# Second edge stage of a graph network kernel: linear maps written edge-major, values weighted on VectorE, the group's maxima transposed right behind the radial weights

## The reference, cut to what matters

```python
ms = src_s[edge_src] + dst_s[edge_dst]
mv = src_v[edge_src] + dst_v[edge_dst]
w1, w2, w3, w4, w5 = split(h @ rw3 + roff)            # radial weights of the edge
o0a, o0b = w1 * ms, w4 * einsum('eud,ed->eu', mv, Y1) / SQ3
o1a, o1b, o1c = (w2 * ms) x Y1, w3 * mv, w5 * cross(mv, Y1) / SQ2
ls, lv = eq_lin([o0a, o0b], [o1a, o1b, o1c], lin_ws, lin_bs, lin_wv)
alpha, vs, vv = ls[:, :64], ls[:, 64:], lv            # 8 heads
a = einsum('ehk,hk->eh', smooth_leaky(alpha), alpha_dot)
a = exp(a - segment_max(a, edge_dst)[edge_dst])
ns = segment_sum(vs * a, edge_dst); nv = segment_sum(vv * a, edge_dst)
```

## Time and profile before

| quantity | value |
|---|---|
| median of three runs | 9799.34 us |
| profiled execution, its own time | 9813.87 us |
| its span | 9812.0 us |
| TensorE busy over the span | 8373.1 us (85%) |
| VectorE busy | 7735.9 us (79%) |
| GpSimd busy | 7372.6 us (75%) |
| ScalarE busy | 4874.4 us (50%) |
| granted TensorE clock, mean | 0.944 |

### The profile page before, as it was taken

One profiled execution on the slowest core, in us unless ns is written; L12 is line 12 of the kernel. 1 busy time (PEld: TensorE's weight loads), 2 busy tenths in 40 slices (PEclk: granted clock), 3 DMA queues, 4 the chain that ended last, 5 costly groups with the idle time before them and its releaser, 6 DMA issues. The chain is left out here.

```text
span 9812.0 us, 193495 instructions
## 1 busy us (share of the span) xinstructions
PE 8373.1 (85%) x35878; PEld 5079.2 (52%) x35878; DVE 7735.9 (79%) x14864; ACT 4874.4 (50%) x9073; POOL 7372.6 (75%) x4571
## 2 busy tenths in 40 slices
PE   0788888888888869999985999999999999998588
PEld 0444444444444422222222777777777777777233
DVE  3177777777777768888886999999999999998465
ACT  0176666666666631121121555555555555555355
POOL 4378888888888878778774888888888888886331
PEclk9599999999999989999997999999999999999799
DMA  5578888888888877778773666666666666665222
GB/s 208 180 161 167 167 168 166 167 167 167 167 167 167 167 213 275 267 271 282 264 270 109 136 137 144 137 143 137 144 138 144 138 142 137 144 137 122 59 70 52
DMA packets 1235170, 1618.04 MB, mean 165 GB/s; under 512 B 222610, under 2 KB 1010589, under 8 KB 1178973
## 3 DMA queue, kind: packets, MB, share of 16 engines
q1 hardware_dynamic: 758950, 1273.86, 40.0%
q0 software_dynamic: 475584, 338.58, 27.1%
HBM read 1533.79 MB, written 444.07 MB: 202 GB/s over the span
## 5 line engine op out<-in xcount | busy, mean ns | idle before, releaser
L1952 POOL DMA_INDIRECT e_m<-TS,e_at x1568 | 2631.8, 1678 | 583.7 <-issue 461.4
L442 POOL DMA_INDIRECT sums<-e_total,e_place x1568 | 2506.9, 1599 | 565.9 <-DMA sums<-e_total,e_place 314.5
L579 PE MATMUL ps<-e_win,e_pick 128*128 128x448 f32 x3136 | 1325.8, 568 | 165.0 <-DVE e_u L476 97.0
L579 PEld LDWEIGHTS ps<-e_win,e_pick 128*128 128x128 f32 x3136 | 612.5, 201 | 921.6 <-issue 864.1
L2275 ACT ACTIVATE e_dT<-ps 128x512 f32<-128x512 f32 x1176 | 660.0, 596 | 495.5 <-PE ps L2149 340.1
L2275 ACT ACTIVATE e_oT<-ps 128x512 f32<-128x512 f32 x784 | 468.9, 598 | 615.1 <-PE ps L2177 373.2
L742 DVE SCALAR_TENSOR_TENSOR r_y<-ps,w_rb,r_rstd 128x512 f32<-128x512 f32 x394 | 295.6, 750 | 579.9 <-issue 533.2
L1096 POOL TENSOR_TENSOR n_zv<-n_zv,n_ast 128x1536 f32<-128x1536 f32 x200 | 703.6, 3518 | 36.6 <-DMA n_zv<-in_x_groups 22.5
L1936 POOL TENSOR_TENSOR e_val<-e_val 128x640 f32<-128x640 f32 x392 | 670.9, 1712 | 61.9 <-ACT e_val L2252 61.9
L2018 DVE TENSOR_TENSOR e_q<-e_row,dstI 128x512 f32<-128x512 int32 x392 | 704.2, 1796 | 13.3 <-PE ps L2163 13.3
L711 PE MATMUL ps<-r_sq,w_avg 128*128 128x512 f32 x788 | 458.1, 666 | 277.4 <-issue 277.4
(11 more groups left out here) (448 smaller groups left out, 19299.8 us busy)
## 6 DMA issues: line engine op xcount, KB each, us to landing
e_win<-T SPq DMA_DIRECT2D x1568, 168.0 KB
n_z<-in_x_groups SPq DMA_DIRECT2D x400, 512.0 KB
n_zv<-in_x_groups SPq DMA_DIRECT2D x800, 192.0 KB
TOT<-e_tot SPq DMA_DIRECT2D x392, 352.0 KB, 2.6
e_row<-in_src_rows SPq DMA_DIRECT2D x98, 1024.0 KB
e_local<-LR SPq DMA_DIRECT2D x196, 512.0 KB
e_row<-in_dst_rows SPq DMA_DIRECT2D x98, 1024.0 KB
e_win<-TD SPq DMA_DIRECT2D x1568, 60.0 KB
```

Of the source, the lines that this page charges most:

```text
L442: pool.indirect_dma_start(sums[c], bass.IndirectOffsetOnAxis(ap=place[:, r % 4, c:c + 1], axis=0), total[:, r % 4, c, 0:MSG0], None, compu ...
L579: pe.matmul(g[:, c, :], pick[:, p, R * c:R * c + R], win[:, s, c, :], start=True, stop=True).then_inc(spread, 1)
L1952: pool.indirect_dma_start(m_[:, r % 4, c, :], None, TS, bass.IndirectOffsetOnAxis(ap=at[:, gp, col:col + 1], axis=0), compute_op=ALU.add). ...
```

## The change

Three things change, all in `layer1_edges`.

1. The maps take the transposed products as the stationary operand and the map's weights as the moving one, tile by tile: four products of 128 columns instead of one of 512. The result is edge-major at once, in two PSUM banks of its own (4 for scalars, 5 for vectors). `turn_back`, its eight transposes and two of ScalarE's five copies are gone. The scalar map now stands between the second and the third `turn`. ScalarE takes tanh and scalar values of step i within step i.
2. `weighted` moves from GpSimd's list to the head of VectorE's step, for step i-6. VectorE's `results` are put in another order.
3. `tops_down` moves from behind the third `turn` to right behind `weights`, ahead of the first `turn`. `weigh_up` moves one step later on ScalarE, from r % 4 == 1 (between copies) to r % 4 == 2 (behind both `keep_far`).

```diff
             def _(pool):
...
-                        if not i.before(8):
-                            weighted(i, 8)
             def _(dve):
...
+                def weighted(i):
+                    j = i.r - 6
+                    slot, gp = j % STEPS, j % STEPS // 4
+                    gate(dve, k)
+                    dve.wait_ge(exped, i.uses(2, j // 4 + 1))
+                    u = val[:, gp, 4 * (slot % 4):4 * (slot % 4) + 4].rearrange("r c (h x) -> r (c h) x", x=SEG)
+                    dve.tensor_tensor(u[:, :, 1:SEG], u[:, :, 1:SEG], bc(u[:, :, 0], SEG - 1, 2), ALU.mult
+                                      ).then_inc(u_ready, 1)
...
+                        if not i.before(6):
+                            weighted(i)
                         if more:
                             sums(after)
                 def map_scalars(i):
                     gate(pe, k)
-                    pe.wait_ge(kept, i.n(5, 2))
-                    pe.matmul(ps[:, bank(i, 5), :], W["la"][:].rearrange("u a h x -> u (a h x)"), dT[:, 0, :], start=True, stop=True
-                              ).then_inc(turned, 1)
+                    pe.wait_ge(kept, i.n(3, 1))
+                    if not i.before(1):
+                        gate(pe, k)
+                        pe.wait_ge(outs, i.n(2))
+                        gate(pe, k)
+                        pe.wait_ge(silued, i.n(2, -1))
+                    for c in range(GT):
+                        last = pe.matmul(scalar_out4[:, c], dT[:, 0, R * c:R * c + R],
+                                         W["la"][:].rearrange("u a h x -> u (a h x)"), start=True, stop=True)
+                    last.then_inc(mapped, 1)
...
-                def turn_back(i, j):
...
+                        if r % 4 == 1 and not i.before(5):
+                            tops_down(i)
                         gate(pe, k)
                         pe.wait_ge(d_ready, i.n(1, 1))
                         turn(i, 0)
                         turn(i, 1)
+                        map_scalars(i)
+                        turn(i, 2)
                         if not i.before(6):
                             totals(i, 0)
-                        turn(i, 2)
-                        if r % 4 == 1 and not i.before(5):
-                            tops_down(i)
-                        map_scalars(i)
+                        map_vectors(i)
                         if not i.before(6):
                             totals(i, 1)
-                        map_vectors(i)
             def _(act):
...
                             keep_far(i.plus(3), 0, far2(i, 0))
                             keep_far(i.plus(3), 1, far2(i, 1))
-                        if not i.before(1):
-                            results(i.plus(-1))
+                        if r % 4 == 2 and not i.before(6):
+                            weigh_up(i.plus(-1))
                         keep(i, 0)
                         keep(i, 1)
+                        keep(i, 2)
+                        results(i)
                         if not i.before(6):
                             keep_totals(i, 0)
-                        keep(i, 2)
-                        keep(i, 3)
-                        if not i.before(6):
                             keep_totals(i, 1)
-                        if r % 4 == 1 and not i.before(5):
-                            weigh_up(i)
-                        keep(i, 4)
```

More of the change, by code:

```diff
@@ L1810, in bank @@
         def bank(i, j):
[L1811 removed]
+            return 2 + (5 * i.r + j) % 2
         def far2(i, half):
@@ L1928, in _ @@
             def _(pool):
-                def weighted(i, back):
-                    j = i.r - back
-                    slot, gp = j % STEPS, j % STEPS // 4
-                    gate(pool, k)
-                    pool.wait_ge(exped, i.uses(2, j // 4 + 1))
-                    u = val[:, gp, 4 * (slot % 4):4 * (slot % 4) + 4].rearrange("r c (h x) -> r (c h) x", x=SEG)
-                    pool.tensor_tensor(u[:, :, 1:SEG], u[:, :, 1:SEG], bc(u[:, :, 0], SEG - 1, 2), ALU.mult
-                                       ).then_inc(u_ready, 1)
                 def body(t):
@@ L1953, in body @@
                                 ap=at[:, gp, col:col + 1], axis=0), compute_op=ALU.add).then_inc(rows_here[r % 4], 16)
-                        if not i.before(8):
-                            weighted(i, 8)
                 passes(pool, body)
-                for r in range(8):
-                    weighted(At(PASSES, r), 8)
             @block.vector
@@ L2026, in results @@
                     dve.wait_ge(outs, i.n(2, 2))
+                    s3 = silu[:, p].rearrange("r c (h x) -> r c h x", h=HEADS)
+                    dve.scalar_tensor_tensor(out=silu[:, p], in0=silu[:, p], scalar=1.5, in1=alpha4, op0=ALU.add, op1=ALU.mult
+                                             ).then_inc(silued, 1)
+                    gate(dve, k)
+                    dve.wait_ge(mapped, i.n(2, 2))
                     for x in range(3):
@@ L2031, in results @@
                     last.then_inc(by_y, 1)
-                    s3 = silu[:, p].rearrange("r c (h x) -> r c h x", h=HEADS)
-                    dve.scalar_tensor_tensor(out=silu[:, p], in0=silu[:, p], scalar=1.5, in1=alpha4, op0=ALU.add, op1=ALU.mult
-                                             ).then_inc(silued, 1)
+                    gate(dve, k)
+                    dve.wait_ge(silued, i.n(2, 1))
+                    dve.tensor_tensor(silu[:, p], silu[:, p], bc(W["ad"][0:R, :], GT, 1), ALU.mult).then_inc(silued, 1)
                     gate(dve, k)
@@ L2109, in _ @@
                 for r in range(5):
+                    weighted(At(PASSES, r))
                     members(At(PASSES, r))
+                weighted(At(PASSES, 5))
             @block.tensor
@@ L2168, in map_scalars @@
                     gate(pe, k)
[L2169 to L2171 removed]
+                    pe.wait_ge(kept, i.n(3, 1))
[8 more added lines that the diff above has]
+                    last.then_inc(mapped, 1)
                 def map_vectors(i):
                     gate(pe, k)
[L2175 to L2183 removed]
+                    pe.wait_ge(kept, i.n(3, 3))
+                    if not i.before(1):
                         gate(pe, k)
@@ L2186, in turn_back @@
                     for c in range(GT):
-                        last = pe.transpose(out4[:, c, 128 * j:128 * j + 128], oT[:, j, R * c:R * c + R], I[:])
+                        pe.matmul(vector_out4[:, c], dT[:, 1, R * c:R * c + R], W["lb"][:].rearrange("u h x -> u (h x)"),
+                                  start=True, stop=False)
+                        last = pe.matmul(vector_out4[:, c], dT[:, 2, R * c:R * c + R],
+                                         W["lc"][:].rearrange("u h x -> u (h x)"), start=False, stop=True)
                     last.then_inc(mapped, 1)
@@ L2237, in _ @@
                 passes(pe, body)
-                for j in range(2):
-                    turn_back(At(PASSES - 1, STEPS - 1), j)
                 logits_up(At(PASSES, 0))
@@ L2325, in _ @@
                 passes(act, body)
-                results(At(PASSES - 1, STEPS - 1))
                 weigh_up(At(PASSES, 1))
```

40 lines of the change are left out of this document (12 added, 28 removed).

## The result

The changed kernel took 10093.15 us (median of four runs, 10083.39 to 10113.04), the kernel before, beside it on the same chip, 9799.04 us. The ratio is 1.0301, with a 95% interval from 1.0283 to 1.0319: 3.0% slower. The forecast had the side right (+0.3%) and the size wrong; 10093 lies above its range of 9700 to 9930.

A forecast was written before the change was run, and what follows sets the result against it. GpSimd's list was taken to bound the kernel at 37.7 us a group; after the change VectorE's 34.44 plus a 3.51 us stall made 38.0. 9813.9 + 29 - 2 = 9841 profiled, forecast 9827 us (+0.3%), range 9700 to 9930.

The forecast's parts named there:

- VectorE's own list, 34.4 us a group: VectorE's work per group of four steps, 4 x 8.13 + 1.92 us, forecast as the longest list, 3.3 less than 37.7.
- the membership back at 0.60 us a slot: `members` on VectorE, 1818 ns in the mean before, was to take 0.60 us without the weighting's reads on GpSimd.
- VectorE blocked by the DMAs (10160): Rival: `members` stays at 1.74 us beside GpSimd's indirect DMAs, 3.4 us a group more, 10160 us; chance 0.05.
- the weight loads open (10240): Rival: 18 more weight loads on TensorE add 2.0 us a step, a group of 42 us, 10240 us; chance 0.04.
- The chain from the scan to the weighting, 8.53 us: From second scan's end through TensorE and ScalarE to the exponential at VectorE: 8.53 us against 5.02 of work, 3.5 us stall.
- It is in time by 0.7 us: TensorE was to reach `tops_down` at 42.9 us, ahead of the next scan's end at 43.6.
- the round behind it: TensorE's way from one step's map to the next step's, summed from its own work to 8.52 us.
- fourth rival: TensorE comes late to the scans, by windows' DMA or slower maps: up to 1 us a group, 9925 us; chance 0.12.
- wait for the exponential: VectorE stands ahead of the weighting in a group's third step until ScalarE's exponential is done: 3.5 us a group.
- first rival: The exponential reaches VectorE within 5.02 us of the scan, group 34.4 us, 9480 us; chance of 9720 or less 0.15.
- GpSimd as the bound of the kernel before: GpSimd's list of four indirect DMAs and one weighting a step was taken as the longest, at 37.7 us a group.

The follow-up runs named there:

- e3: Changed kernel with SyncE's store of the totals one step later (step i-7 instead of i-6): 9968.60 us, ratio 1.0156 to the kernel before.
- e13: Changed kernel with both halves of the totals, and ScalarE's copy of the first, back in their places of before: 9891.01 us, ratio 1.0048.
- e6: Changed kernel with the weighting just ahead of `weigh` and the store of the totals one step later: 9688.71 us, ratio 0.9863 to the kernel before.
- e5: Kernel before with only the weighting moved from GpSimd to the head of VectorE's step, for step i-6: 9649.61 us, ratio 0.9828.
- e12: Changed kernel with weighting just ahead of `weigh`, totals' store one step later, exponential back in the group's second step: 9686.52 us, ratio 0.9872.
- e14: Changed kernel with the totals back in their places of before, weighting just ahead of `weigh`, and store one step later: 9721.73 us, ratio 0.9875.
- e9: Kernel before with only the edge-major maps and their step order; weighting on GpSimd, maxima and exponential in their old places: 10030.05 us, ratio 1.0225.
- e4: Changed kernel with the weighting back on GpSimd, for step i-8: 9943.43 us, ratio 1.0129 to the kernel before.

## Why the prediction was wrong

- **VectorE's own list, 34.4 us a group: right within 0.3.** In the window 5430 to 9100 of the changed profile VectorE was busy 3064.55 us in 357 weightings' time, 34.3 us a group. From start to start it is 40.90 - 5.68 - 0.53 = 34.7 us, the group less the waits at the weighting and the shift. The list leaves out the idle time that stands once in a turn of the loop, 70.2 / 94.5 = 0.7 us a group ahead of L1980 before and 0.4 ahead of the weighting now. The largest term in it, the membership back at 0.60 us a slot, came out (682 ns, 680 forecast). The weighting took 823 ns (810 forecast). The two rivals that hung on these, VectorE blocked by the DMAs (10160) and the weight loads open (10240), did not occur: twelve products of the vector map took from 7404.75 to 7406.09, 0.11 us each, as forecast. The rule that the prediction took from the Trainium skill (TensorE: Matmul & The Clock Gate, "The mechanism"), that a weight load overlaps running products only when the row groups differ, is not borne out by these rows; the same section also lets a load into the background weight buffer run ahead, which the prediction left out. The Trainium skill's rule on two SBUF inputs beside a GpSimd instruction that reads SBUF (SBUF — State Buffer, "Who interferes with whom") agrees with the membership's 1818 and 682 ns.
- **The chain from the scan to the weighting, 8.53 us: right where its start was.** The group at 7380 has 8.52 us, but it is one of four in 84 in which TensorE is in time. From the transpose of the maxima to the weighting are 8.6 us in the mean of the changed kernel and of e3, and the forecast had 8.53 - 0.15 = 8.38. e13's +0.48% beside the forecast's +0.3% is not the same kernel, as said above.
- **"It is in time by 0.7 us": this step failed.** I brought TensorE from the third step's map at 18.46 us to `tops_down` at 42.9, in 24.4 us, by adding up its own work at full speed, and let its loads be there. The timelines have 28.1 us in the mean of the changed kernel and 26.5 in e3. So two terms stood at nothing. The first is the loads. The working counted the totals' half of 0.57 us in the chain, but not who waits for it: the copy, SyncE's store, and behind the store the windows and hidden rows of the next steps. I followed the moved steps through the lists of TensorE, ScalarE and VectorE and left out SyncE's. With the loads late TensorE came 2.5 us behind the scan at 7419.67, and 2.3 us in the mean, instead of 0.7 ahead. e3 cures this and takes 40.90 - 39.31 = 1.6 of the 2.9 us by which the group was missed. The second is the slow products behind the wait for `silued`. The forecast had that wait, but counted the round behind it at 8.52 us, where e3 has 9.9. It is read from rows and not tested alone.
- **The size of the fourth rival: too small.** "By a wait for the windows' DMA or by slower maps" named the place, at 1 us a group at most. Of the 2.9 us (40.90 against 38.0), 5.25 - 3.5 = 1.7 are the longer wait for the exponential and 0.5 the new wait at the shift, both of which follow from TensorE's lateness; 0.4 are the idle time once in a turn of the loop. The rest, 0.2 to 0.3, lies in small gaps. As I read it the lateness feeds itself: it lengthens the chain to the exponential, VectorE's stall makes TensorE wait for `silued`, and behind such a wait the products take up to twice as long. I had priced it as one delay.
- **The first rival (9480, the wait hidden) did not occur in the changed kernel.** e6 hides it and reaches 36.46 us, not 34.4, since GpSimd's DMAs became slower (below).
- **GpSimd as the bound of the kernel before: right in effect.** Taking its weighting off alone (e5) gives 1.7%. The group went to 35.99, not to VectorE's 34.4. TensorE and VectorE are both busy 96% there, and which of them bounds it wasn't tried.

## What to carry to other kernels

When an operation is moved, follow its result past the engine that consumes it: to the store that waits for the copy, and to the loads that are queued behind the store. A margin of 0.7 us in 38, summed up from busy times, is no margin; price the miss with what it makes late in turn, not as one delay. Run the parts of a change apart before judging it: here one part held a gain of 1.7% and another a loss of 2.3%. And ask of a part that loses whether it is the idea or the order that came with it: with the totals back in their places, 2.5 of the 3.0 points were gone.

## What the runs showed of the hardware

- **TensorE after a wait.** In the changed kernel it did nothing from 7433 to 7435, and the granted clock of the next stretch is 0.69 (last row; the columns are those of the window above):

```profile
7419.00:7423.00 4.00, 3.81 (x13) 3.42 (x14) 3.51 (x11) 0.00 (x0) 3.39 (x3) 0.57 0.41 93
7429.00:7433.00 4.00, 3.61 (x25) 3.33 (x24) 1.83 (x5) 2.57 (x7) 1.67 (x2) 1.00 0.90 298
7433.00:7435.00 2.00, 0.00 (x0) 0.00 (x0) 1.97 (x6) 0.37 (x1) 1.70 (x2) 1.00 0.47 73
7435.00:7439.00 4.00, 3.59 (x20) 3.59 (x21) 4.00 (x13) 1.57 (x4) 2.99 (x2) 0.69 0.54 95
```

  Four transposes took 0.98 us in it, where four take 0.60 in the third step's usual place, and 0.69 lies between the two levels of 1.2 and 2.4 GHz. The eight products of the radial weights took 3.17 us instead of 1.68 after the two waits for DMAs (1.17 and 1.03 us), at a clock of 0.57 (first row), so 1.5 us more. In e3 the round behind a wait of 2.90 us took 9.94 us, and the next, from 7407.97 to 7416.67, 8.70: 1.2 us more.
- **GpSimd's indirect DMAs take longer when nothing holds GpSimd up.** Their mean is 1639 to 1760 ns in the kernels in which GpSimd weights values or waits over 500 us for `keep_far`, and 1981, 1961 and 1868 ns in e6, e12 and e14, where that wait is 33, 57 and 225 us; single ones reach 3.73 us in e6. Whether the queue behind them sets that pace, or something that runs beside them, was not tried.
- **A small lock depends on phase.** The same weighting on GpSimd cost VectorE's membership a mean of 1.1 us before; in e9 it cost two lines 0.9 and 0.65 us, with the same instructions, and in e4 it hardly touched the membership (700 ns).
